# Two layer-norm tiles at a time instead of one on VectorE: subtract, subtract, multiply, multiply

## The chip, the cores and the metric

The kernel runs on all 8 cores of one Trainium2 chip. Each core computes 2048 of the 16384 tokens and talks to no other core; the cores share only the memory behind them. The metric is the device time of the slowest core in microseconds (us).

## The reference

The input is x, 16384 tokens of 4096 features (float32). Two sub-layers follow each other, each wrapped in two layer norms (sandwich form):

```
x = x + layernorm( layernorm(x) @ weight.T + bias )
x = x + layernorm( ffn(layernorm(x)) )
ffn(y) = y @ W_base.T + b_base + 2 * sum over experts of w[t,e] * (y @ lora_A[e].T) @ lora_B[e].T
```

The expert weights w are a softmax over 8 router logits of which the two largest are kept and made to sum to one. The two products with 4096x4096 matrices are nearly all of the arithmetic.

## The kernel before

Features lie on the 128 partitions, tokens along the free dimension. A core works through its 2048 tokens in four chunks of 512 (`ch`), and a chunk is 32 tiles of 128 features by 512 tokens (`k`). `xt` holds x in float32, `u` the normalized input of a product in bf16, `zb` the product in bf16. Each chunk goes through these stages, one after the other:

1. **A, first statistics.** ACT issues four loads of `xt`, 8 tiles each (line 227), copies and squares each tile (lines 233, 234), and PE sums over partitions with a column of ones. The load of the group g of the next chunk waits until POOL has made the output tile 8g+7 of this chunk, since that add reads `xt` (lines 220, 221).
2. **A, apply (lines 266 to 273).** The mean and the inverse deviation are spread over the partitions as `mbc_bf` and `ibc_bf`. VectorE (DVE) subtracts and multiplies tile by tile through two small buffers `ybf0`, `ybf1` and writes `u`. The first product's matmuls of its first output tile wait for `u` tile by tile (line 339).
3. **B, product.** 32 output tiles of 32 matmuls each (line 340), weights through two buffers `wb`. In chunk 0 the float32 weights are cast on the way in and written back to memory as bf16; later chunks read the bf16 copy. ACT copies and squares each result (lines 324, 325).
4. **C, apply and first residual (lines 364 to 374).** For each tile DVE subtracts (`zb` minus mean into `ybf`, line 367) and multiplies in place (line 370), and POOL (GpSimd) adds the result to `xt` (line 373). ACT squares the new `xt` (line 382) for the next statistics.
5. **D, apply (lines 416 to 423).** As in A, into `u`, for the router (line 432) and the second product. Stages A and D are called the u stages below.
6. **E, product.** As in B (line 527), with the low-rank part.
7. **F, apply, second residual and store (lines 549 to 567).** Subtract (line 553), multiply (line 556), add on POOL into one of two float32 buffers `ost` (line 559), and a store of 256 KB by the queue of SP (line 563). With it run the loads and statistics of the next chunk's stage A.

All order between and within engines is by semaphores written by hand. On DVE, a multiply waits for the subtract whose result it reads. In stage C the subtract of tile k waits for the add of tile k-2, in stage F for the add and for the store of tile k-2. POOL's own queue also issues the weight loads, in program order with its adds; the first two of a product stand behind the 32 adds of the stage before it.

Of the kernel before, what the change touches and what calls it, by code (L numbers as in the profile page):

```python
# [14 lines left out]
C = 512  # L15
NCH = TOK // C
KT = D // 128
# [6 lines left out]
def build_nc():  # L24
# [10 lines left out]
    outd = nc.dram_tensor("out", [D, TOK], F32, kind="ExternalOutput").ap()  # L35
# [3 lines left out]
    cnt = {"t": 0, "v": 0, "s": 0, "g": 0, "gc": 0,  # L39
           "x": [0, 0, 0, 0], "w": [0, 0], "o": [0, 0], "wsc": [0, 0]}  # L40

    def emit(e, fn):
        ops[e].append(fn)

    def wait(e, sem, val):
        if val > 0:
            emit(e, lambda eng, sem=sem, val=val: eng.wait_ge(sem, val))

    with ExitStack() as _es:
        xt = _es.enter_context(nc.sbuf_tensor("xt", [128, KT * C], F32))  # L50
        u = _es.enter_context(nc.sbuf_tensor("u", [128, KT * C], BF16))
        zb = _es.enter_context(nc.sbuf_tensor("zb", [128, OC * C], BF16))
# [14 lines left out]
        ybf0 = _es.enter_context(nc.sbuf_tensor("ybf0", [128, C], BF16))  # L67
        ybf1 = _es.enter_context(nc.sbuf_tensor("ybf1", [128, C], BF16))
        mbc_bf = _es.enter_context(nc.sbuf_tensor("mbc_bf", [128, C], BF16))
        ibc_bf = _es.enter_context(nc.sbuf_tensor("ibc_bf", [128, C], BF16))  # L70
# [36 lines left out]
        s_v = _es.enter_context(nc.semaphore("s_v"))  # L107
# [12 lines left out]
        s_gc = _es.enter_context(nc.semaphore("s_gc"))  # L120
# [4 lines left out]
        ost = [ost0, ost1]  # L125
# [3 lines left out]
        s_o = [s_o0, s_o1]  # L129
# [10 lines left out]
        def v_inc(fn):  # L140
            cnt["v"] += 1
            emit("V", lambda v, fn=fn: fn(v).then_inc(s_v, 1))
            return cnt["v"]

        def s_inc(fn):
            cnt["s"] += 1
            emit("S", lambda s, fn=fn: fn(s).then_inc(s_s, 1))
            return cnt["s"]

        def g_inc(fn):  # L150
            cnt["gc"] += 1
            emit("G", lambda g, fn=fn: fn(g).then_inc(s_gc, 1))
            return cnt["gc"]
# [25 lines left out]
        nout = 0  # L179
# [33 lines left out]
        f6k = {}  # L213
        for ch in range(NCH):
            t_pair = {}
            s_pair = {}
            for k in range(KT):
                if k % 8 == 0:
                    g = k // 8
# [43 lines left out]
                wait("V", s_gc, f6k[KT - 1])  # L263
            uk = {}
            yb = [ybf0, ybf1]
            for k in range(KT):
                if k >= 2:
                    wait("V", s_v, uk[k - 2])
                r = v_inc(lambda v, k=k: v.tensor_sub(yb[k % 2][:],  # L269
                                                      xt[:, k * C:(k + 1) * C], mbc_bf[:]))  # L270
                wait("V", s_v, r)
                uk[k] = v_inc(lambda v, k=k: v.tensor_mul(u[:, k * C:(k + 1) * C],  # L272
                                                          yb[k % 2][:], ibc_bf[:]))
            vv_u_done = cnt["v"]
            vv_apply_bank_free = cnt["v"]

# [83 lines left out]
            wait("V", s_o[0], cnt["o"][0])  # L360
            wait("V", s_o[1], cnt["o"][1])
            c3k = {}
            yb = [ybf0, ybf1]
            for k in range(KT):
                if k >= 2:
                    wait("V", s_gc, c3k[k - 2])
                r = v_inc(lambda v, k=k: v.tensor_sub(yb[k % 2][:],  # L367
                                                      zb[:, k * C:(k + 1) * C], mbc_bf[:]))
                wait("V", s_v, r)
                vc = v_inc(lambda v, k=k: v.tensor_mul(yb[k % 2][:], yb[k % 2][:],  # L370
                                                       ibc_bf[:]))
                wait("G", s_v, vc)
                c3k[k] = g_inc(lambda g, k=k: g.tensor_add(  # L373
                    xt[:, k * C:(k + 1) * C], xt[:, k * C:(k + 1) * C], yb[k % 2][:]))
            vv_c_done = cnt["v"]
            vv_apply_bank_free = cnt["v"]

# [22 lines left out]
            r = v_inc(lambda v: v.tensor_scalar_mul(row_a[:], ps_sqq[0:1, :], 1.0 / D))  # L400
            wait("V", s_v, r)
            r = v_inc(lambda v: v.tensor_mul(row_b[:], row_m[:], row_m[:]))
            wait("V", s_v, r)
            r = v_inc(lambda v: v.tensor_sub(row_a[:], row_a[:], row_b[:]))
# [4 lines left out]
            r = s_inc(lambda s: s.activation(row_b[:], row_a[:], AF.Ln))  # L409
# [3 lines left out]

            wait("V", s_s, bc_d)
            wait("V", s_gc, c3k[KT - 1])
            for k in range(KT):
                if k >= 2:
                    wait("V", s_v, uk[k - 2])
                r = v_inc(lambda v, k=k: v.tensor_sub(yb[k % 2][:],  # L419
                                                      xt[:, k * C:(k + 1) * C], mbc_bf[:]))  # L420
                wait("V", s_v, r)
                uk[k] = v_inc(lambda v, k=k: v.tensor_mul(u[:, k * C:(k + 1) * C],  # L422
                                                          yb[k % 2][:], ibc_bf[:]))
            vv_u_done = cnt["v"]
            vv_apply_bank_free = cnt["v"]

# [21 lines left out]
            for tt in range(4):  # L448
# [17 lines left out]
                r2 = v_inc(lambda v, tt=tt: v.reduce_max(m2s[:, tt:tt + 1], l2t[:],  # L466
                                                         axis=AX.X))
# [78 lines left out]
            vv_stats_read = va  # L546
            bc_f = bc_pair(row_zm, va, sa, vv_apply_bank_free, s_free_need=vv_u_done)
            wait("V", s_s, bc_f)
            for k in range(KT):
                if k >= 2:  # L550
                    wait("V", s_o[k % 2], cnt["o"][k % 2])
                    wait("V", s_gc, f6k[k - 2])
                r = v_inc(lambda v, k=k: v.tensor_sub(yb[k % 2][:],  # L553
                                                      zb[:, k * C:(k + 1) * C], mbc_bf[:]))
                wait("V", s_v, r)
                vc = v_inc(lambda v, k=k: v.tensor_mul(yb[k % 2][:], yb[k % 2][:],  # L556
                                                       ibc_bf[:]))
                wait("G", s_v, vc)
                f6k[k] = g_inc(lambda g, k=k: g.tensor_add(  # L559
                    ost[k % 2][:], yb[k % 2][:], xt[:, k * C:(k + 1) * C]))  # L560
                wait("Y", s_gc, f6k[k])
                def ostore(y, ch=ch, k=k):
                    return y.dma_start(outd[k * 128:(k + 1) * 128, ch * C:(ch + 1) * C],
                                       ost[k % 2][:]).then_inc(s_o[k % 2], 16)
                emit("Y", ostore)
                nout += 1
                cnt["o"][k % 2] += 16
            vv_f6_done = cnt["v"]
            sv_zb_free = cnt["v"]
            vv_apply_bank_free = cnt["v"]  # L570
# [84 lines left out]
```

## Time and profile before

| | before |
|---|---|
| median of 3 runs | 3453.99 us (3449.34 to 3455.17) |
| the profiled execution's own time | 3449.01 us |
| its span, first to last instruction (slowest core) | 3447.2 us |
| spans of the 8 cores | 3421.6 to 3447.2 us |
| PE busy | 2386.2 us (69%) |
| DVE busy | 658.0 us (19%) |
| ACT busy | 544.5 us (16%) |
| POOL busy | 441.2 us (13%) |

Busy shares are averages over stages that are limited by different things, so they don't say what a change in one stage is worth. For that one reads the chain of work that ended last, and the timeline of the stage.

### The profile page before, as it was taken

What the parts mean: (1) busy time and instruction counts of PE and PEld (TensorE: products, weight loads), DVE (VectorE), ACT (ScalarE), POOL (GpSimd) and SP (SyncE); (2) the same over time, 40 slices, a digit from 0 to 9 for tenths busy, and PEclk for the clock granted to TensorE, in tenths of its full rate; (3) what the DMA queues carried; (4) which work ended last, traced back from release to release, by engine and by line L of the source; (5) the groups of instructions that cost most, each with busy time, mean ns of one, the idle gap of its engine ahead of it and who ended that gap; (6) DMA issues with size and microseconds to landing.
All of it is one profiled execution on the core that took longest, in us unless ns stands there. A gap on an engine that the chain in (4) does not pass through costs nothing.

```text
span 3447.2 us, 27405 instructions; the slowest of 8 cores (3421.6 to 3447.2 us)
## 1 busy us (share of the span) xinstructions
PE 2386.2 (69%) x10016; PEld 971.7 (28%) x10204; DVE 658.0 (19%) x1243; ACT 544.5 (16%) x1001; POOL 441.2 (13%) x521
## 2 busy tenths in 40 slices
PE   2577853788713998279943899459962599639990
PEld 0133311333300443034410344124420144214440
DVE  0400037000034000820022300640012400370003
ACT  3110121011122111211113011301112111211110
POOL 0000022000030000400022000400013000220004
PEclk7698975899955999589975799669985699759995
DMA  7298932799742333024334234013425144103332
GB/s 173 60 201 200 204 91 51 165 201 209 179 136 84 126 140 112 26 71 144 136 105 143 89 139 145 32 38 137 141 86 171 64 139 141 61 26 126 139 114 98
DMA packets 81891, 417.12 MB, mean 121 GB/s; under 512 B 7648, under 2 KB 7776, under 8 KB 40544
## 3 DMA queue, kind: packets, MB, share of 16 engines
q0 software_dynamic: 37472, 279.04, 30.6%
q1 hardware_dynamic: 27648, 102.77, 7.6%
q10 hardware_dynamic: 16640, 33.56, 3.0%
q8 instruction: 83, 1.36, 0.2%
q14 instruction: 48, 0.39, 0.0%
HBM read 383.98 MB, written 102.76 MB: 141 GB/s over the span
## 4 chain that ended last, share of the span: by engine, by line
PE 48%; DMA 24%; DVE 15%; issue 6%; ACT 3%; POOL 2%; another core or an unknown queue 1%; DVEq 0%; ACTq 0%; POOLq 0%; SPq 0%
PE P L340 21%; PE P L527 21%; DMA wsc<-wb 6%; DMA out<-ost 5%; DMA wb<-wF 5%; DMA wb<-wA 5%; DVE ybf L370 4%; DMA xt<-xT 3%; DVE ybf L419 3%; DVE ybf L269 3%; POOL ost L559 2%; DVE ybf L367 2%; PE ps_sq L306 1%; DVE ybf L556 1%; DVE ybf L553 1%
## 5 line engine op out<-in xcount | busy, mean ns | idle before, releaser
L340 PE MATMUL P<-u,wb 128*128 128x512 bf16 x4004 | 972.1, 394 | 156.6 <-DVE u L272 82.5
L527 PE MATMUL P<-u,wb 128*128 128x512 bf16 x4012 | 930.9, 389 | 74.6 <-DMA wb<-wF 62.5
L340 PEld LDWEIGHTS P<-u,wb 128*128 128x128 bf16 x4096 | 404.4, 100 | 718.5 <-issue 282.8
L527 PEld LDWEIGHTS P<-u,wb 128*128 128x128 bf16 x4096 | 404.5, 100 | 588.1 <-issue 137.9
L324 ACT CAST zb<-P 128x512 bf16<-128x512 f32 x256 | 149.8, 585 | 2019.3 <-PE P L345 790.1
L184 DVE TENSOR_SCALAR row_zm<-ps_sq 1x512 f32<-1x512 f32 x8 | 5.4, 679 | 2163.7 <-PE ps_sqq L312 2163.7
L297 POOL DMA_DIRECT2D wb<-wsc x192 | 101.5, 529 | 1699.4 <-PE P L345 840.8
L242 PE MATMUL ps_sq<-xbf,ones 128*1 128x512 bf16 x128 | 60.1, 569 | 354.2 <-ACT sq L234 354.2
L559 POOL TENSOR_TENSOR ost<-ybf,xt 128x512 f32<-128x512 bf16 x128 | 150.0, 1172 | 328.5 <-DVE ybf L556 328.5
L373 POOL TENSOR_TENSOR xt<-xt,ybf 128x512 f32<-128x512 f32 x128 | 153.3, 1198 | 169.4 <-DVE ybf L370 165.6
L325 ACT ACTIVATE sq<-P 128x512 bf16<-128x512 f32 x256 | 154.4, 603 | 0.0
L370 DVE TENSOR_TENSOR ybf<-ybf,ibc_bf 128x512 bf16<-128x512 bf16 x128 | 148.3, 1158 | 14.8 <-DVE ybf L367 1.8
L389 PE MATMUL ps_sqq<-sq,ones 128*1 128x512 bf16 x64 | 37.4, 585 | 160.2 <-ACT sq L382 160.2
L233 ACT CAST xbf<-xt 128x512 bf16<-128x512 f32 x128 | 77.5, 605 | 290.4 <-DMA xt<-xT 290.0
L432 PE MATMUL ps_mix<-rTs,u 128*128 128x8 bf16 x512 | 31.5, 167 | 132.3 <-DVE u L422 132.3
L242 PEld LDWEIGHTS ps_sq<-xbf,ones 128*1 128x1 bf16 x128 | 7.3, 80 | 408.6 <-issue 408.6
L553 DVE TENSOR_TENSOR ybf<-zb,mbc_bf 128x512 bf16<-128x512 bf16 x128 | 64.3, 503 | 242.5 <-DMA out<-ost 199.9
L382 ACT ACTIVATE sq<-xt 128x512 bf16<-128x512 f32 x128 | 80.7, 630 | 134.8 <-POOL xt L373 125.9
L269 DVE TENSOR_TENSOR ybf<-xt,mbc_bf 128x512 bf16<-128x512 f32 x128 | 87.8, 686 | 28.0 <-ACT ibc_bf L210 27.9
L419 DVE TENSOR_TENSOR ybf<-xt,mbc_bf 128x512 bf16<-128x512 f32 x128 | 87.9, 687 | 26.9 <-ACT ibc_bf L210 26.9
L234 ACT ACTIVATE sq<-xt 128x512 bf16<-128x512 f32 x128 | 79.9, 624 | 0.0
L306 PE MATMUL ps_sq<-zb,ones 128*1 128x512 bf16 x256 | 65.5, 378 | 11.0 <-ACT sq L325 11.0
(87 smaller groups left out, 989.0 us busy)
## 6 DMA issues: line engine op xcount, KB each, us to landing
wb<-wsc POOLq DMA_DIRECT2D x192, 1056.0 KB, 5.3
wsc<-wb SPq DMA_DIRECT2D x64, 1056.0 KB, 7.7
wb<-wA POOLq DMA_DIRECT2D x32, 1056.0 KB, 11.2
wb<-wF POOLq DMA_DIRECT2D x32, 1056.0 KB, 11.3
xt<-xT ACTq DMA_DIRECT2D x16, 2048.0 KB, 10.3
out<-ost SPq DMA_DIRECT2D x128, 256.0 KB, 2.4
aTs<-aT POOLq DMA_DIRECT2D x1, 1024.0 KB, 15.6
bTs<-bT POOLq DMA_DIRECT2D x1, 1024.0 KB, 22.1
```

The lines of the kernel that those rows point to most:

```text
L269: r = v_inc(lambda v, k=k: v.tensor_sub(yb[k % 2][:], xt[:, k * C:(k + 1) * C], mbc_bf[:]))
L297: emit("G", lambda g, mat=mat, oc=oc, par=par: g.dma_start(wb[par][:], wsc[mat, oc]).then_inc(s_w[par], 16))
L306: t_run(lambda t, j=j: t.matmul(ps_sq[0:1, :], ones128[:, 0:1], zb[:, j * C:(j + 1) * C], start=(j == 0), stop=(j == OC - 1)))
L324: s_inc(lambda s, po=po: s.copy(zb[:, po * C:(po + 1) * C], P[po % 2][:]))
L325: ev[po] = s_inc(lambda s, po=po: s.activation(sq[po % 4][:], P[po % 2][:], AF.Square))
L340: t_run(lambda t, oc=oc, k=k: t.matmul(P[oc % 2][:], wb[oc % 2][:, k * 128:(k + 1) * 128], u[:, k * C:(k + 1) * C], start=(k == 0), stop=F ...
L370: vc = v_inc(lambda v, k=k: v.tensor_mul(yb[k % 2][:], yb[k % 2][:], ibc_bf[:]))
L373: c3k[k] = g_inc(lambda g, k=k: g.tensor_add(xt[:, k * C:(k + 1) * C], xt[:, k * C:(k + 1) * C], yb[k % 2][:]))
L419: r = v_inc(lambda v, k=k: v.tensor_sub(yb[k % 2][:], xt[:, k * C:(k + 1) * C], mbc_bf[:]))
L527: t_run(lambda t, oc=oc, k=k: t.matmul(P[oc % 2][:], wb[oc % 2][:, k * 128:(k + 1) * 128], u[:, k * C:(k + 1) * C], start=(k == 0), stop=F ...
L553: r = v_inc(lambda v, k=k: v.tensor_sub(yb[k % 2][:], zb[:, k * C:(k + 1) * C], mbc_bf[:]))
L559: f6k[k] = g_inc(lambda g, k=k: g.tensor_add(ost[k % 2][:], yb[k % 2][:], xt[:, k * C:(k + 1) * C]))
```

## The change

In the four apply loops the 32 tiles are taken in 16 pairs (`kp`). DVE subtracts both tiles of a pair (into `ybf0` and `ybf1`), waits for the second subtract, and multiplies both. Before the next pair it waits for what used the two buffers last: in the u stages for the pair's second multiply; in stage C for POOL's add of the pair's second tile; in stage F for that add and for the stores of both tiles. The instructions, their shapes and their buffers are the same; their order on DVE and the waits differ. The order on POOL and SP is the same.

```diff
 # stages A and D (two loops of this form)
-            for k in range(KT):
-                if k >= 2:
-                    wait("V", s_v, uk[k - 2])
-                r = v_inc(lambda v, k=k: v.tensor_sub(yb[k % 2][:],
-                                                      xt[:, k * C:(k + 1) * C], mbc_bf[:]))
-                wait("V", s_v, r)
-                uk[k] = v_inc(lambda v, k=k: v.tensor_mul(u[:, k * C:(k + 1) * C],
-                                                          yb[k % 2][:], ibc_bf[:]))
+            for kp in range(0, KT, 2):
+                if kp >= 2:
+                    wait("V", s_v, uk[kp - 1])
+                v_inc(lambda v, kp=kp: v.tensor_sub(yb[0][:],
+                                                    xt[:, kp * C:(kp + 1) * C], mbc_bf[:]))
+                r2 = v_inc(lambda v, kp=kp: v.tensor_sub(
+                    yb[1][:], xt[:, (kp + 1) * C:(kp + 2) * C], mbc_bf[:]))
+                wait("V", s_v, r2)
+                uk[kp] = v_inc(lambda v, kp=kp: v.tensor_mul(
+                    u[:, kp * C:(kp + 1) * C], yb[0][:], ibc_bf[:]))
+                uk[kp + 1] = v_inc(lambda v, kp=kp: v.tensor_mul(
+                    u[:, (kp + 1) * C:(kp + 2) * C], yb[1][:], ibc_bf[:]))
 # stage F (stage C has the same form, without the stores and their waits)
-            for k in range(KT):
-                if k >= 2:
-                    wait("V", s_o[k % 2], cnt["o"][k % 2])
-                    wait("V", s_gc, f6k[k - 2])
-                r = v_inc(lambda v, k=k: v.tensor_sub(yb[k % 2][:],
-                                                      zb[:, k * C:(k + 1) * C], mbc_bf[:]))
-                wait("V", s_v, r)
-                vc = v_inc(lambda v, k=k: v.tensor_mul(yb[k % 2][:], yb[k % 2][:],
-                                                       ibc_bf[:]))
-                wait("G", s_v, vc)
-                f6k[k] = g_inc(lambda g, k=k: g.tensor_add(
-                    ost[k % 2][:], yb[k % 2][:], xt[:, k * C:(k + 1) * C]))
...
+            for kp in range(0, KT, 2):
+                if kp >= 2:
+                    wait("V", s_o[0], cnt["o"][0])
+                    wait("V", s_o[1], cnt["o"][1])
+                    wait("V", s_gc, f6k[kp - 1])
+                v_inc(lambda v, kp=kp: v.tensor_sub(yb[0][:],
+                                                    zb[:, kp * C:(kp + 1) * C], mbc_bf[:]))
+                r2 = v_inc(lambda v, kp=kp: v.tensor_sub(
+                    yb[1][:], zb[:, (kp + 1) * C:(kp + 2) * C], mbc_bf[:]))
+                wait("V", s_v, r2)
+                vc0 = v_inc(lambda v: v.tensor_mul(yb[0][:], yb[0][:], ibc_bf[:]))
+                vc1 = v_inc(lambda v: v.tensor_mul(yb[1][:], yb[1][:], ibc_bf[:]))
+                for k, vc in ((kp, vc0), (kp + 1, vc1)):
+                    wait("G", s_v, vc)
+                    f6k[k] = g_inc(lambda g, k=k: g.tensor_add(
+                        ost[k % 2][:], yb[k % 2][:], xt[:, k * C:(k + 1) * C]))
...
```

## Rows read from the trace of the kernel before

**Rows 1.** Spans and mean granted TensorE clock, the slowest core:
```profile
core 6: 3447.2 us, clock 0.814
```
**Rows 2.** Page: the chain that ended last, by engine; then waits (total, times, longest):
```profile
PE 48%; DMA 24%; DVE 15%; issue 6%; ACT 3%; POOL 2%; another core or an unknown queue 1%; DVEq 0%; ACTq 0%; POOLq 0%; SPq 0%
...
DVE ybf L553 <- DMA out<-ost: 199.9, 98, 6.5
...
POOL xt L373 <- DVE ybf L370: 165.6, 121, 31.7
...
PE ps_mix L432 <- DVE u L422: 132.3, 128, 2.8
```
**Rows 3.** Engines in stage C of chunk 1 (busy PE, PEld, DVE, ACT, POOL; PEclk; DMA):
```profile
1378.00:1431.00 53.00, 15.17 (x30) 1.70 (x30) 47.95 (x64) 19.69 (x32) 37.99 (x32) 0.50 0.00 1
```
**Rows 4.** Timeline, stage A apply of chunk 1 (start us, us, engine line):
```profile
1108.23 0.68 DVE L269 TENSOR_TENSOR ybf<-xt,mbc_bf 128x512 bf16<-128x512 f32 x1
...
1108.46 0.59 PE L340 MATMUL P<-u,wb 128*128 128x512 bf16 x1 [0.55 <-DVE u L272]
1109.02 0.42 DVE L272 TENSOR_TENSOR u<-ybf,ibc_bf 128x512 bf16<-128x512 bf16 x1
1109.36 0.69 DVE L269 TENSOR_TENSOR ybf<-xt,mbc_bf 128x512 bf16<-128x512 f32 x1
```
**Rows 5.** Timeline, stage C of chunk 1, its start and its end:
```profile
1378.39 0.43 DVE L367 TENSOR_TENSOR ybf<-zb,mbc_bf 128x512 bf16<-128x512 bf16 x1 [6.76 <-ACT ibc_bf L210]
1378.92 0.43 DVE L370 TENSOR_TENSOR ybf<-ybf,ibc_bf 128x512 bf16<-128x512 bf16 x1
1379.27 0.42 DVE L367 TENSOR_TENSOR ybf<-zb,mbc_bf 128x512 bf16<-128x512 bf16 x1
1379.50 1.19 POOL L373 TENSOR_TENSOR xt<-xt,ybf 128x512 f32<-128x512 f32 x1 [27.97 <-DVE ybf L370]
1379.79 1.19 DVE L370 TENSOR_TENSOR ybf<-ybf,ibc_bf 128x512 bf16<-128x512 bf16 x1
1380.79 0.63 ACT L382 ACTIVATE sq<-xt 128x512 bf16<-128x512 f32 x1 [2.63 <-POOL xt L373]
1380.90 0.41 DVE L367 TENSOR_TENSOR ybf<-zb,mbc_bf 128x512 bf16<-128x512 bf16 x1
1381.12 1.20 POOL L373 TENSOR_TENSOR xt<-xt,ybf 128x512 f32<-128x512 f32 x1 [0.42 <-DVE ybf L370]
...
1430.17 1.15 POOL L373 TENSOR_TENSOR xt<-xt,ybf 128x512 f32<-128x512 f32 x1 [0.42 <-PE ps_sqq L392]
1431.27 1.09 POOL L297 DMA_DIRECT2D wb<-wsc  x2
```
**Rows 6.** Stage C's adds in chunk 1 (ns min/median/max, first to last start us):
```profile
L373 POOL TENSOR_TENSOR xt<-xt,ybf x32: 1150/1201/1203, 1379.5 to 1430.2; 128x512 f32<-128x512 f32 x32
```
**Rows 7.** Timeline, stage F of chunk 1: an add and the subtract after its store:
```profile
1768.66 1.16 POOL L559 TENSOR_TENSOR ost<-ybf,xt 128x512 f32<-128x512 bf16 x1 [1.91 <-DVE ybf L556]
...
1772.68 0.43 DVE L553 TENSOR_TENSOR ybf<-zb,mbc_bf 128x512 bf16<-128x512 bf16 x1 [2.06 <-DMA out<-ost]
```
**Rows 8.** Stage F's adds in the four chunks (as in group 6):
```profile
L559 POOL TENSOR_TENSOR ost<-ybf,xt x32: 1154/1157/1428, 959.7 to 1050.4; 128x512 f32<-128x512 bf16 x32
...
L559 POOL TENSOR_TENSOR ost<-ybf,xt x32: 1154/1158/1420, 1764.0 to 1854.1; 128x512 f32<-128x512 bf16 x32
...
L559 POOL TENSOR_TENSOR ost<-ybf,xt x32: 1154/1158/1396, 2562.9 to 2662.8; 128x512 f32<-128x512 bf16 x32
...
L559 POOL TENSOR_TENSOR ost<-ybf,xt x32: 1154/1157/1202, 3368.8 to 3443.1; 128x512 f32<-128x512 bf16 x32
```
**Rows 9.** The stores of stage F of chunk 3, issue to landing:
```profile
DMA to landing us min/median/max: 2.1/2.2/2.7
```
**Rows 10.** A load of `xt` (timeline), and a piece of the chain in chunk 1:
```profile
1782.70 0.43 ACTq L227 DMA_DIRECT2D xt<-xT  x1
...
1785.22 6.76 DMA out<-ost
```

More of the change, by code:

```diff
@@ L362, in build_nc @@
             c3k = {}
-            yb = [ybf0, ybf1]
-            for k in range(KT):
-                if k >= 2:
-                    wait("V", s_gc, c3k[k - 2])
-                r = v_inc(lambda v, k=k: v.tensor_sub(yb[k % 2][:],
-                                                      zb[:, k * C:(k + 1) * C], mbc_bf[:]))
-                wait("V", s_v, r)
-                vc = v_inc(lambda v, k=k: v.tensor_mul(yb[k % 2][:], yb[k % 2][:],
-                                                       ibc_bf[:]))
-                wait("G", s_v, vc)
-                c3k[k] = g_inc(lambda g, k=k: g.tensor_add(
-                    xt[:, k * C:(k + 1) * C], xt[:, k * C:(k + 1) * C], yb[k % 2][:]))
+            for kp in range(0, KT, 2):
+                if kp >= 2:
+                    wait("V", s_gc, c3k[kp - 1])
+                v_inc(lambda v, kp=kp: v.tensor_sub(yb[0][:],
[7 more added lines that the diff above has]
+                    wait("G", s_v, vc)
+                    c3k[k] = g_inc(lambda g, k=k: g.tensor_add(
+                        xt[:, k * C:(k + 1) * C], xt[:, k * C:(k + 1) * C],
+                        yb[k % 2][:]))
             vv_c_done = cnt["v"]
@@ L415, in build_nc @@
             wait("V", s_gc, c3k[KT - 1])
[L416 to L423, printed above, removed]
+            for kp in range(0, KT, 2):
+                if kp >= 2:
+                    wait("V", s_v, uk[kp - 1])
+                v_inc(lambda v, kp=kp: v.tensor_sub(yb[0][:],
+                                                    xt[:, kp * C:(kp + 1) * C], mbc_bf[:]))
+                r2 = v_inc(lambda v, kp=kp: v.tensor_sub(
+                    yb[1][:], xt[:, (kp + 1) * C:(kp + 2) * C], mbc_bf[:]))
+                wait("V", s_v, r2)
+                uk[kp] = v_inc(lambda v, kp=kp: v.tensor_mul(
+                    u[:, kp * C:(kp + 1) * C], yb[0][:], ibc_bf[:]))
+                uk[kp + 1] = v_inc(lambda v, kp=kp: v.tensor_mul(
+                    u[:, (kp + 1) * C:(kp + 2) * C], yb[1][:], ibc_bf[:]))
             vv_u_done = cnt["v"]
@@ L548, in build_nc, with ostore @@
             wait("V", s_s, bc_f)
-            for k in range(KT):
-                if k >= 2:
-                    wait("V", s_o[k % 2], cnt["o"][k % 2])
-                    wait("V", s_gc, f6k[k - 2])
[L553 to L558, printed above, removed]
-                f6k[k] = g_inc(lambda g, k=k: g.tensor_add(
-                    ost[k % 2][:], yb[k % 2][:], xt[:, k * C:(k + 1) * C]))
[L561 to L567, printed above, removed]
+            for kp in range(0, KT, 2):
+                if kp >= 2:
+                    wait("V", s_o[0], cnt["o"][0])
+                    wait("V", s_o[1], cnt["o"][1])
+                    wait("V", s_gc, f6k[kp - 1])
+                v_inc(lambda v, kp=kp: v.tensor_sub(yb[0][:],
+                                                    zb[:, kp * C:(kp + 1) * C], mbc_bf[:]))
+                r2 = v_inc(lambda v, kp=kp: v.tensor_sub(
+                    yb[1][:], zb[:, (kp + 1) * C:(kp + 2) * C], mbc_bf[:]))
+                wait("V", s_v, r2)
+                vc0 = v_inc(lambda v: v.tensor_mul(yb[0][:], yb[0][:], ibc_bf[:]))
+                vc1 = v_inc(lambda v: v.tensor_mul(yb[1][:], yb[1][:], ibc_bf[:]))
+                for k, vc in ((kp, vc0), (kp + 1, vc1)):
+                    wait("G", s_v, vc)
+                    f6k[k] = g_inc(lambda g, k=k: g.tensor_add(
+                        ost[k % 2][:], yb[k % 2][:], xt[:, k * C:(k + 1) * C]))
+                    wait("Y", s_gc, f6k[k])
+                    def ostore(y, ch=ch, k=k):
+                        return y.dma_start(
+                            outd[k * 128:(k + 1) * 128, ch * C:(ch + 1) * C],
+                            ost[k % 2][:]).then_inc(s_o[k % 2], 16)
+                    emit("Y", ostore)
+                    nout += 1
+                    cnt["o"][k % 2] += 16
```

## The prediction

> **What bounds the kernel now.** I first read the spans of the cores: the slowest is core 6, and all rows are its own [rows 1]. Then the chain that ended last: PE has only half of it, DMA and DVE most of the rest [rows 2]. So the kernel runs in phases: in the products PE is the bound, and between them PE waits for the layer norms. The waits name the phases that the change touches. POOL waits 165.6 us for DVE's multiply in stage C, DVE waits 199.9 us for stores in stage F, and PE waits 132.3 us for `u` at the router [rows 2]. In stage C's window nothing covers this: PE is at clock 0.50, its lower level (1.2 GHz), with 15 of 53 us busy on small sums, DMA moves nothing, and DVE and POOL alternate [rows 3]. All four apply loops lie on the path, so what a loop loses, the kernel loses. The rest of the reading is the timeline of each loop, from which I build the loop anew in the new order.
>
> **Three prices of DVE.** A DVE instruction that needs nothing from the one before it starts 0.08 us before that one's end: the multiply at 1378.92 is followed by the subtract at 1379.27, 0.35 us from start to start. One that needs its result starts 0.10 us after the end: 1378.39 to 1378.92, 0.53 us [rows 5]. So a true wait on the previous instruction costs 0.18 us. The same in the u stages: 0.79 us from a float32 subtract to its multiply, 0.34 us from there to the next subtract [rows 4].
>
> **The u stages (A and D, 8 loops).** Before, a pair of tiles takes 2 x (0.79 + 0.34) = 2.26 us. After, second subtract: the trace has no two float32 subtracts in a row; by the overlap of 0.08 it starts 0.60 us after the first. Then 0.79 to the first multiply, 0.34 to the second, and now the next pair waits for that multiply: 0.53. Sum 2.26 us. The pairing removes one true wait per pair (between a subtract and its multiply) and adds one (between the second multiply and the next subtract), since only two buffers exist. Gain: zero; only the last pair has no next one, 0.19 us per loop. PE's matmul on a new tile runs at the low clock (0.59 us for one [rows 4]; its 512 columns alone are 0.43 at 1.2 GHz), longer than the 0.34 between the two multiplies, which takes back about 0.09 at the end. Together -0.1 x 8, about -1 us. Bounds: if two subtracts don't overlap, +0.19 x 16 pairs x 8 loops = +24 us; nothing can gain more than the -1.5 of the last pairs unless a wait is free.
>
> The Trainium skill (VectorE: DVE Perf Modes, "The DRAIN you can't avoid") says that leaving semaphores out between DVE instructions saves nothing, because each drains the pipeline anyway. By it the second subtract would start 0.53 and not 0.35 us after the first, and the change would cost some 23 us more in stages C and F together. The trace disagrees: 0.35 against 0.53 in two neighbouring steps [rows 5].
>
> **Stage C (4 loops).** Before, DVE and POOL run in a chain: multiply ends, add starts 0.14 us later, meanwhile the next subtract runs; the next multiply is recorded from 1379.79 for 1.19 us, of which only the last 0.29 lie behind the add; then the next add [rows 5]. Per tile 1.20 + 0.43; the 31 steps take 50.7 us [rows 6], 3.27 us per pair. The subtract is hidden under this; the multiply nearly so. After, DVE may not start a pair before POOL has made both adds, so nothing hides any longer. One pair:
> - from the add's end to the subtract: 0.10, as ACT needs it (add ends 1380.69, ACT starts 1380.79) [rows 5];
> - subtract to subtract 0.35, subtract to multiply 0.53, multiply to first add 0.58 (1378.92 to 1379.50) = 1.46; the second multiply starts 0.35 after the first, as the subtract does now, and ends before the first add does;
> - first add 1.20, of which 0.05 is waiting for the DVE instruction begun before it (an undisturbed one takes 1.15), second add right behind: POOL's next instruction starts 1.10 after an add of 1.15 began [rows 5], so 1.15 to the second's start and 1.15 to its end = 2.30.
>
> Together 3.86 us against 3.27. From first to last add 15 x 3.86 + 1.15 = 59.0 us against 50.7: +8.4 per loop, +33.5 in all (chunk 0's loop is 0.3 shorter before). Behind the adds in POOL's queue stand the first two weight loads of stage E; they move with the stage and still have the whole of stage D before the first matmul needs them. ACT's squares take 0.63 and keep up. Bounds: if the first add must wait for the whole second multiply, 0.15 more per pair; if the second add starts later by a handshake of 0.14, as much again; below, 0.10 less if DVE starts with no delay. That is 27 to 50 us.
>
> **Stage F (4 loops).** Chunk 3's loop has no loads beside it: 74.3 us for 31 steps [rows 8], 4.79 us per pair. A buffer's loop is subtract to multiply 0.53, multiply to add 0.58, add 1.16, and then the store; what is left for the store with its issue and both handshakes is 4.79 - 2.27 = 2.52 us. It fits the landing of 2.2 us [rows 9], and the single case beside other stores from 1769.82 to 1772.68, 2.86 us [rows 7]. Before, two such loops run interleaved. After, both wait for the later store, and the two adds stand one behind the other: 1.46 + 2.30 + 2.52 = 6.28 us per pair. Loop: 15 x 6.28 + 1.15 = 95.4 us against 74.3: +21.0 for chunk 3. With 2.86 for the store it would be +26, with 2.35 it would be +18.5.
>
> Chunks 0 to 2 have three loads of `xt` inside the loop; their loops take 90.7, 90.1 and 99.9 us [rows 8], so a load costs (90.4 - 74.3) / 3 = 5.4 us before in the first two. The mechanism is in one row: a store issued 2.5 us behind a load takes 6.76 us and lands 9.3 after the load's issue [rows 10]. After, the pair behind the load makes its adds later: 2.5 + 1.46 + 2.30 = 6.3 us after the load's issue, and its last store would land at 8.8 anyway. So it loses 0.5 us at least, and 4.3 if it also takes 6.76. I take 2 per load, since only the tail of the load is met: 95.4 + 6 = 101.4, and 7 more in chunk 2, where some other contention adds about 10 now. Against 90.7, 90.1 and 99.9: +10.7, +11.3, +8.5 = +30.3 (the third with 108.4). With no loss and nothing in chunk 2 it would be +5; with the old price 5.4 and chunk 2's whole excess +63.
>
> The loads of the next chunk move with the adds; the last one is issued after the last add in either kernel, and the statistics after it are as before. Chunk 0's weight casts and write-backs, and all products, are shifted and not changed.
>
> **Sum.** -1 + 33.5 + 21.0 + 30.3 = +83.8 us. On the profiled execution, 3449.0 us (span 3447.2), that gives 3532.8; the median of the runs lies 5.0 above it, so 3454.0 + 83.8 = 3537.8, rounded to 3538: slower by 2.4%.
>
> **Rivals.**
> 1. *The port between DVE and POOL is freed, and the kernel gets faster.* Now nearly every multiply of stage C stretches beside an add, 1.19 for 0.43 us (POOL waits for one 121 times) [rows 2, 5]; with DVE silent during the adds that stretching goes, about 0.75 x 121 = 90 us of DVE's busy time. For it to bring time, the add itself must get faster, because the stretched part lies beside an add. Place: the adds of stages C and F. The pairing costs 84 us over 256 adds, so it decides at 0.33 us per add, 1.15 down to 0.82; at 0.80 the kernel would take 3538 - 0.35 x 256 = 3448. Against it: the shortest of all adds, some of them with DVE idle, takes 1.15 [rows 6, 8]. The Trainium skill (SBUF — State Buffer, "Who interferes with whom") has the port as an exclusive lock whose loser is blocked; the row of the multiply that ends 0.29 behind the add agrees. By that rule the first add of a pair would wait out the second multiply, which makes the change dearer by 19 us.
> 2. *Stage F hides it.* If stores bunched in pairs meet the loads less and a load costs nothing, and the wait for the store shrinks to the shortest, 2.35, each loop takes 15 x 6.11 + 1.15 = 92.8 us; chunks 0 to 2 then lose 2.1 and 2.7 and gain 7.1, chunk 3 loses 18.5, about +16 together, and with stage C's 33.5 the time is 3503. For it: the third loop's 99.9 us shows how much is contention. Against: the stores' wait is now serial for both buffers.
> 3. *Everything at its dear end.* No overlap of float32 subtracts (+24), old price of loads (+33): 3454 + 84 + 57 = 3595. Against it: the overlap shows in every bf16 step.
> 4. *No change that can be measured*: it would need DVE's waits in C and F to be met already. They can't be: the add waited for is the last that POOL made.
>
> **How the numbers follow.** Forecast as summed with its bounds, 3510 to 3585: 0.80. Rival 2 (3485 to 3510): 0.10. Rival 3 (over 3585): 0.07. Rival 1: 0.02 faster. Rival 4: 0.01. The range that leaves out no more than two in ten is that of the forecast, 3510 to 3585. 0.2% is about what a measurement of this kernel can tell from no change. Faster 0.02, same 0.01, slower 0.97.
>
> **What would show it.** In the timeline of stage C, pairs of adds back to back with a gap of about 1.55 us between pairs, a pair every 3.9 us, and multiplies of 0.43. In stage F, a pair every 6.3 us and over 2.4 us from the second add's end to the subtract. In the u stages the same 36 us. All three products unchanged. Wrong if adds of a pair are apart, if the first-to-last add of a stage C loop is below 55 us, if a float32 subtract starts 0.79 and not 0.60 after the one before, or if a load in stage F costs its old 5.4 us.

## The result, and the profile after

| | before | after |
|---|---|---|
| median | 3454.58 us (10 runs) | 3551.16 us (10 runs) |
| ratio after to before, 95% interval | | 1.027 (1.0242 to 1.0299) |
| the profiled execution's own time | 3449.01 us | 3553.48 us |
| its span, slowest core | 3447.2 us, core 6 | 3551.9 us, core 1 |

The medians differ by 96.6 us, and the ratio gives 93; 83.8 were forecast. Some executions of any of these kernels run some per cent longer, with the cores of one die at a lower granted clock, and the medians take them in while the ratios and their intervals leave them out. The top of the page after, with the busy times and the chain that ended last:

```profile
span 3551.9 us, 27097 instructions; the slowest of 8 cores (3518.9 to 3551.9 us)
## 1 busy us (share of the span) xinstructions
PE 2385.1 (67%) x10204; PEld 971.6 (27%) x10204; DVE 531.1 (15%) x1243; ACT 544.5 (15%) x1001; POOL 434.1 (12%) x521
...
PE 48%; DMA 22%; DVE 14%; issue 7%; POOL 5%; ACT 3%; DVEq 0%; POOLq 0%; ACTq 0%; SPq 0%
```

DVE has the same 1243 instructions and is busy for 531.1 us instead of 658.0, while the kernel takes longer. Most of the 127 us were instructions that stretched beside an add and were hidden there, the multiplies of stage C above all. This row of the page before has them at 1158 ns each; after, none takes over 0.43 us, which alone is 94 us less:

```profile
L370 DVE TENSOR_TENSOR ybf<-ybf,ibc_bf 128x512 bf16<-128x512 bf16 x128 | 148.3, 1158 | 14.8 <-DVE ybf L367 1.8
```

POOL's share of the chain rose from 2% [rows 2] to 5%: its adds no longer run beside the work of DVE for the next tile.

The waits after (total, times, longest), to be read against [rows 2]:

```profile
DVE ybf L565 <- DMA out<-ost: 318.8, 60, 8.0
...
POOL xt L379 <- DVE ybf L375: 205.2, 61, 32.2
...
DVE ybf L370 <- POOL xt L379: 134.4, 60, 2.6
...
PE ps_mix L443 <- DVE u L431: 119.5, 64, 3.4
```

DVE's wait for stores grew from 199.9 to 318.8 us, and there is a wait that the kernel before did not have: DVE for POOL's second add in stage C, 60 times 2.2 us. The timeline of stage C of chunk 1 after, one pair and the start of the next:

```profile
1424.99 0.43 DVE L370 TENSOR_TENSOR ybf<-zb,mbc_bf 128x512 bf16<-128x512 bf16 x1 [2.22 <-POOL xt L379]
1425.34 0.42 DVE L372 TENSOR_TENSOR ybf<-zb,mbc_bf 128x512 bf16<-128x512 bf16 x1
...
1425.86 0.42 DVE L375 TENSOR_TENSOR ybf<-ybf,ibc_bf 128x512 bf16<-128x512 bf16 x1
...
1426.20 0.42 DVE L376 TENSOR_TENSOR ybf<-ybf,ibc_bf 128x512 bf16<-128x512 bf16 x1
1426.43 2.31 POOL L379 TENSOR_TENSOR xt<-xt,ybf 128x512 f32<-128x512 f32 x2 [1.54 <-DVE ybf L375]
...
1428.84 0.42 DVE L370 TENSOR_TENSOR ybf<-zb,mbc_bf 128x512 bf16<-128x512 bf16 x1 [2.22 <-POOL xt L379]
```

Four DVE instructions of 0.42 us run while POOL stands idle for 1.54 us; then two adds back to back, 2.31 us, while DVE stands idle for 2.22. A pair every 3.85 us. In [rows 5] POOL's gap is 0.42 us per tile. The u stages, of which this is the start of stage D in chunk 1, and one step of stage F in chunk 3:

```profile
1494.72 0.69 DVE L426 TENSOR_TENSOR ybf<-xt,mbc_bf 128x512 bf16<-128x512 f32 x1 [6.72 <-ACT ibc_bf L210]
1495.33 0.69 DVE L428 TENSOR_TENSOR ybf<-xt,mbc_bf 128x512 bf16<-128x512 f32 x1
1496.12 0.43 DVE L431 TENSOR_TENSOR u<-ybf,ibc_bf 128x512 bf16<-128x512 bf16 x1
1496.46 0.42 DVE L433 TENSOR_TENSOR u<-ybf,ibc_bf 128x512 bf16<-128x512 bf16 x1
1496.98 0.69 DVE L426 TENSOR_TENSOR ybf<-xt,mbc_bf 128x512 bf16<-128x512 f32 x1
```

```profile
3455.43 2.32 POOL L574 TENSOR_TENSOR ost<-ybf,xt 128x512 f32<-128x512 bf16 x2 [28.63 <-DVE ybf L570]
...
3460.12 0.42 DVE L565 TENSOR_TENSOR ybf<-zb,mbc_bf 128x512 bf16<-128x512 bf16 x1 [4.50 <-DMA out<-ost]
...
3461.55 2.32 POOL L574 TENSOR_TENSOR ost<-ybf,xt 128x512 f32<-128x512 bf16 x2 [3.81 <-DVE ybf L570]
```

In the u stages two float32 subtracts start 0.61 us apart, and the next pair starts 0.52 after the second multiply: 2.26 us per pair, as before. In stage F 2.37 us pass between the end of the adds and the next subtract, and a pair comes every 6.12 us. Last, the adds of one stage C and of the four stages F (ns min/median/max, first to last start in us), against [rows 6, 8]:

```profile
L379 POOL TENSOR_TENSOR xt<-xt,ybf x32: 1144/1152/1201, 1422.6 to 1482.0; 128x512 f32<-128x512 f32 x32
```

```profile
L574 POOL TENSOR_TENSOR ost<-ybf,xt x32: 1147/1179/1212, 974.5 to 1095.3; 128x512 f32<-128x512 bf16 x32
...
L574 POOL TENSOR_TENSOR ost<-ybf,xt x32: 1147/1158/1213, 1814.8 to 1916.4; 128x512 f32<-128x512 bf16 x32
...
L574 POOL TENSOR_TENSOR ost<-ybf,xt x32: 1147/1160/1215, 2632.6 to 2738.9; 128x512 f32<-128x512 bf16 x32
...
L574 POOL TENSOR_TENSOR ost<-ybf,xt x32: 1147/1157/1208, 3455.4 to 3547.9; 128x512 f32<-128x512 bf16 x32
```

From first to last add, stage C takes 59.4 us against 50.7. Stage F on core 1: 120.8, 101.6, 106.3 and 92.5 us. Core 1 is the slowest core after, core 6 was the slowest before, so the loops of stage F are better compared over all cores. Each number here is the last add's start minus the first's, as in the rows, taken for each of the 8 cores and averaged (us):

| stage F | chunk 0 | 1 | 2 | 3 | sum |
|---|---|---|---|---|---|
| before | 89.2 | 89.8 | 93.1 | 75.8 | 347.9 |
| after | 109.7 | 104.1 | 103.2 | 94.0 | 410.9 |

Stage F costs 63.0 us more on an average core. The four loops of stage C, taken in the same way, sum to 236.7 us against 202.5, 34.2 more (58.9 to 59.5 each, against 50.4 to 50.7). Together that is 97.2 us. The products are unchanged: a matmul takes 395 and 388 ns on average in the two of them, against 394 and 389.

### The profile page after: what moved, and what is told of

Same layout as the page of the kernel before. It is cut to its first block, busy times and chain, and to the rows that moved or that the text cites. A ratio compares the mean times of both kernels' runs of the same rounds, so it can differ in the third digit from the quotient of the medians.

```text
span 3551.9 us, 27097 instructions; the slowest of 8 cores (3518.9 to 3551.9 us)
## 1 busy us (share of the span) xinstructions
PE 2385.1 (67%) x10204; PEld 971.6 (27%) x10204; DVE 531.1 (15%) x1243; ACT 544.5 (15%) x1001; POOL 434.1 (12%) x521
## 4 chain that ended last, share of the span: by engine, by line
PE 48%; DMA 22%; DVE 14%; issue 7%; POOL 5%; ACT 3%; DVEq 0%; POOLq 0%; ACTq 0%; SPq 0%
PE P L538 21%; PE P L344 20%; DMA wsc<-wb 5%; DMA out<-ost 5%; DMA wb<-wF 5%; DMA wb<-wA 4%; DMA xt<-xT 3%; POOL xt L379 3%; POOL ost L574 3%; PE ps_sq L310 1%; DVE ybf L426 1%; DVE ybf L269 1%; DVE ybf L271 1%; DVE ybf L428 1%; PE ps_sqq L314 1%
## 5 line engine op out<-in xcount | busy, mean ns | idle before, releaser
L565 DVE TENSOR_TENSOR ybf<-zb,mbc_bf 128x512 bf16<-128x512 bf16 x64 | 27.2, 425 | 345.4 <-DMA out<-ost 318.8
L290 POOL DMA_DIRECT2D wb<-wA x32 | 16.9, 531 | 436.3 <-PE P L349 324.4
L443 PEld LDWEIGHTS ps_mix<-rTs,u 128*128 128x128 bf16 x512 | 23.6, 104 | 144.2 <-issue 144.2
## 6 DMA issues: line engine op xcount, KB each, us to landing
wb<-wF POOLq DMA_DIRECT2D x32, 1056.0 KB, 11.3
```

## The experiments

Nine of the eleven kernels were also timed beside the kernel before on the same chip; ratios are to that. Of the two of experiment 6 there is one execution each. Every kernel keeps the whole computation. The code cuts leave out lines that did not change or that repeat the same edit.

**1. Each part alone.** Three kernels take the changed loops in the u stages only (A and D), in stage C only, and in stage F only; the other loops are those before.

> Only the u stages (A and D) are paired; C and F are as before. Theory (one true wait removed per pair, one added): a pair of tiles takes 2.26 us as before, each loop about 0.2 us shorter, the kernel within 2 us of before (3453). Rival A (float32 subtracts don't overlap): +0.19 x 16 x 8 = +24 us, 3479. Rival B (fewer handshakes are a gain in themselves: a wait on DVE's own last multiply costs nothing): -0.19 x 16 x 8 = -24 us, 3431.

> Only stage C is paired. Theory (nothing of DVE lies under POOL's adds any longer): a pair every 3.86 us, first to last add 59 us against 50.7, kernel +33.5 us (3488). Rival (freed port makes the adds faster): adds below 1.10 us each and a kernel of 3454 or less.

> Only stage F is paired. As predicted: chunk 3's loop 95 us against 74, the others 101 to 108, +51 us (3506). By the traces since seen (loops summed over the 8 cores: +63 us a core, with loops of 100 to 120 us in chunk 0): +60 to +70, 3515 to 3524. Rival (stage F hides it in the landing times): below +20.

| kernel | median | ratio (95% interval) | in us by the ratio |
|---|---|---|---|
| u stages only | 3451.89 | 0.999 (0.9958 to 1.0021) | -3 |
| stage C only | 3485.57 | 1.0094 (1.0073 to 1.0115) | +32.5 |
| stage F only | 3516.28 | 1.0182 (1.0156 to 1.0208) | +63 |

The parts add up to +92, and the whole change measured +93 by its ratio. The u stages are worth nothing. That is what the theory said, and it speaks against both rivals (+24 and -24 us): the interval reaches from -14 to +7 us, and the 2.26 us per pair in the trace is sharper. With stage C alone the adds of chunk 1 read

```profile
L376 POOL TENSOR_TENSOR xt<-xt,ybf x32: 1140/1152/1252, 1386.8 to 1446.0; 128x512 f32<-128x512 f32 x32
```

The loop takes 59.2 us. The shortest add takes 1.14 us where it took 1.15 before, and the middle one 1.15 where it took 1.20 [rows 6]: with DVE silent an add gains about 0.05 us, where the rival needed 0.33.

**2. The changed order, but each buffer waited for on its own.**

```diff
 # on the changed kernel; stage F in the same way with its stores
             for kp in range(0, KT, 2):
                 if kp >= 2:
-                    wait("V", s_gc, c3k[kp - 1])
+                    wait("V", s_gc, c3k[kp - 2])
                 v_inc(lambda v, kp=kp: v.tensor_sub(yb[0][:], ...
+                if kp >= 2:
+                    wait("V", s_gc, c3k[kp - 1])
                 r2 = v_inc(lambda v, kp=kp: v.tensor_sub(
```

> The changed kernel, but in C and F each subtract of a pair waits only for what used its own buffer last (the first no longer waits for the second tile's add and store). Theory: the first subtract leaves the path but stays blocked under the second add, so stage C gains about 0.24 us per pair (first to last add 55.5 us) and stage F 0.35 per pair: -35 us against the changed kernel, 3516, still 60 us slower than before. Rival (the doubled wait alone is the loss, and the order of the instructions is not): back to the time before, 3454.

Measured 3517.06 us, ratio 1.0182 (1.0154 to 1.021). That is 34 us less than the changed kernel by the medians and 30 by the ratios, where 35 were expected. From its timeline:

```profile
1423.80 2.31 POOL L382 TENSOR_TENSOR xt<-xt,ybf 128x512 f32<-128x512 f32 x2 [1.29 <-DVE ybf L378]
1425.11 1.29 DVE L371 TENSOR_TENSOR ybf<-zb,mbc_bf 128x512 bf16<-128x512 bf16 x1 [1.11 <-POOL xt L382]
...
1426.32 0.41 DVE L375 TENSOR_TENSOR ybf<-zb,mbc_bf 128x512 bf16<-128x512 bf16 x1
...
1427.40 2.31 POOL L382 TENSOR_TENSOR xt<-xt,ybf 128x512 f32<-128x512 f32 x2 [1.29 <-DVE ybf L378]
```

The first subtract may now start when the first add is done, but it stretches to 1.29 us and ends 0.29 after the second add. So a pair takes 3.60 us, 0.25 less, and stage F sums to 385.4 us over the four loops on an average core, 25 less. Two thirds of the loss stay (63 of 93 us by the ratios), so the doubled wait is the smaller part of it. In the rows above POOL still waits 1.29 us between two pairs of adds: for the last 0.29 of the blocked subtract, for the second subtract and for the first multiply. With two buffers none of that can be done earlier.

**3. The changed order over four buffers.** All four loops take pairs; `ybf` and `ost` get four buffers each, and the waits go back two pairs.

```diff
 # against the changed kernel, stage C; in stage F the stores' waits go back in the same way
+                b0, b1 = yb4[kp % 4], yb4[kp % 4 + 1]
-                if kp >= 2:
-                    wait("V", s_gc, c3k[kp - 1])
+                if kp >= 4:
+                    wait("V", s_gc, c3k[kp - 3])
```

> The changed order (subtract, subtract, multiply, multiply) in all four loops, but with four ybf and four ost buffers, so that a pair waits for what the pair before the last one did. Theory (the loss is the reuse of two buffers within one step, not the order): u stages 2.07 us per pair instead of 2.26, -24 us against before; stage C back to about 3.3 us per pair (51 us per loop), bound by POOL and DVE taking turns; stage F no longer waits for landings, about 3.3 to 3.6 us per pair, 25 us or more shorter per loop than before. Kernel 3320 to 3360. Rival (the order itself is the loss: a pair's adds come in a bunch behind four DVE instructions): stage C stays at 58 to 60 us per loop and the kernel above 3440.

Ratio 0.9703 (0.9595 to 0.9811); the two executions that it stands on took 3347 and 3379 us, and the second is the one in the trace. Its stage C in the slowest core, core 4 (DVE, then POOL, then the 32 adds of chunk 2):

```profile
1362.26 1.38 DVE L382 TENSOR_TENSOR ybf<-zb,mbc_bf 128x512 bf16<-128x512 bf16 x1
1363.56 1.37 DVE L384 TENSOR_TENSOR ybf<-zb,mbc_bf 128x512 bf16<-128x512 bf16 x1
1365.04 0.42 DVE L387 TENSOR_TENSOR ybf<-ybf,ibc_bf 128x512 bf16<-128x512 bf16 x1
1365.38 0.42 DVE L388 TENSOR_TENSOR ybf<-ybf,ibc_bf 128x512 bf16<-128x512 bf16 x1
```

```profile
1362.15 2.50 POOL L391 TENSOR_TENSOR xt<-xt,ybf 128x512 f32<-128x512 f32 x2 [0.96 <-DVE ybf L387]
1365.60 2.50 POOL L391 TENSOR_TENSOR xt<-xt,ybf 128x512 f32<-128x512 f32 x2 [0.95 <-DVE ybf L387]
```

```profile
L391 POOL TENSOR_TENSOR xt<-xt,ybf x32: 1147/1226/1332, 2123.6 to 2176.4; 128x512 f32<-128x512 f32 x32
```

Both subtracts of the next pair lie under the adds again, all but the last 0.28 us. The pair takes 3.45 us and the loop 52.8 (52.7 to 53.0 on every core and in every chunk), against 50.7 before and 59.4 after. So in stage C the order alone costs about 2 us per loop; the other 6.4 come from two buffers for a pair, which leave nothing to prepare. The u stages take 2.07 us per pair, as expected. The stage F loops take 69.1, 68.8, 68.8 and 55.1 us on an average core. Here the order is not tested by itself, since the four `ost` buffers alone change much: with them and the old order experiment 5 has 60.1, 58.4, 58.6 and 51.4 us. Whether the 4 to 10 us between the two come from the order or from the store's wait, which stays on DVE here, no run separates.

**4. Where the waits are, seen from the other side.** If a true wait on DVE's previous instruction costs 0.18 us, staggering must gain what pairing over two buffers can't: the subtract of the next tile is put between a subtract and its multiply. The kernel before, u stages only (instructions shortened to words):

```diff
-            for k in range(KT):
-                if k >= 2:
-                    wait("V", s_v, uk[k - 2])
-                r = v_inc(subtract tile k into yb[k % 2])
-                wait("V", s_v, r)
-                uk[k] = v_inc(multiply yb[k % 2] into u, tile k)
+            for k in range(KT + 1):
+                if k < KT:
+                    if k >= 4:
+                        wait("V", s_v, uk[k - 4])
+                    rk[k] = v_inc(subtract tile k into yb4[k % 4])
+                if k >= 1:
+                    wait("V", s_v, rk[k - 1])
+                    uk[k - 1] = v_inc(multiply yb4[(k - 1) % 4] into u, tile k - 1)
```

> The kernel before, but in the u stages the subtract of tile k+1 is issued ahead of the multiply of tile k, over four buffers; C and F as before. Theory (each true wait on DVE's previous instruction costs 0.18 us, and pairing over two buffers only moved it): no wait is true any longer, 0.60 + 0.34 = 0.94 us per tile instead of 1.13, -6 us per loop, -48 us: 3406. Rival (waits cost nothing, DVE is bound by its instructions): 3454.

```profile
1104.75 0.70 DVE L274 TENSOR_TENSOR ybf<-xt,mbc_bf 128x512 bf16<-128x512 f32 x1
1105.35 0.43 DVE L279 TENSOR_TENSOR u<-ybf,ibc_bf 128x512 bf16<-128x512 bf16 x1
1105.69 0.70 DVE L274 TENSOR_TENSOR ybf<-xt,mbc_bf 128x512 bf16<-128x512 f32 x1
1106.29 0.43 DVE L279 TENSOR_TENSOR u<-ybf,ibc_bf 128x512 bf16<-128x512 bf16 x1
```

0.60 + 0.34 = 0.94 us per tile, as expected. From first subtract to last multiply a loop takes 29.7 us against 35.9, which is 50 us in the eight loops. The two executions that the ratio stands on took 3397 and 3399 us, and the trace's own is 52 us below the kernel before; the ratio is 0.9804 (0.9708 to 0.9899), that is -68 us, with an interval from -101 to -35 that holds the 48 expected. Shown: with the same instructions, a wait for the instruction just before costs 0.18 us, and a wait for one further back, which is over by then, costs nothing that these rows can tell.

**5. Stage F's store.** The kernel before, with the store's wait moved from DVE's subtract to POOL's add, and the same with four `ost` buffers.

```diff
                 if k >= 2:
-                    wait("V", s_o[k % 2], cnt["o"][k % 2])
                     wait("V", s_gc, f6k[k - 2])
...
                 wait("G", s_v, vc)
+                wait("G", s_o[k % 2], cnt["o"][k % 2])
```

> The kernel before, but in stage F POOL's add waits for the store of two tiles ago, and not DVE's subtract. Theory (the loop of a buffer, subtract 0.53 + multiply 0.58 + add 1.16 + store 2.52, sets stage F): subtract and multiply leave it, 3.7 us per pair instead of 4.79, chunk 3's loop 57 us against 74, the kernel -50 to -70 us: 3384 to 3404. Rival (the stores' transfer itself is the bound): 3454.

> As f_poolwait, with four ost buffers. Theory: the landing leaves the path altogether, stage F runs at stage C's pace of 3.27 us per pair, 51 us per loop in chunk 3 and somewhat more beside the loads: 3340 to 3370. If the landings still bound it beside the loads of xt: 3370 to 3395.

Measured 3399.74 us, ratio 0.9793 (0.9697 to 0.9888), and 3344.27 us, ratio 0.9648 (0.9587 to 0.9709). The four loops sum to 290.5 and 228.6 us on an average core, against 347.9. Stage F of chunk 3 with four buffers:

```profile
L565 POOL TENSOR_TENSOR ost<-ybf,xt x32: 1152/1157/1387, 3284.8 to 3336.2; 128x512 f32<-128x512 bf16 x32
```

The loop takes 51.4 us, near stage C's pace of 50.7. So before the change the landing of a store was on the path of nearly every tile, and the stage had 23 us per loop to give back even without loads.

**6. Stage F without the loads.** In the kernel before and in the changed one, all loads of `xt` are issued after the last add (`f6k[8 * g + 7]` becomes `f6k[KT - 1]` at line 221). Only the loops are read.

> The kernel before, with all four loads of xt of the next chunk issued after the last add of stage F instead of three of them inside it. Only stage F's loops are read (the kernel as a whole gets slower, the loads no longer lie beside the stage). Theory: the loads are what makes the loops of chunks 0 to 2 longer than chunk 3's: all four loops take 73 to 76 us from first to last add, against 87 to 100 now. Rival (other cores' traffic): chunks 0 to 2 stay 5 us or more longer than chunk 3.

> The changed kernel, with the loads of xt issued after stage F in the same way. Theory: all four loops 92 to 94 us, so that without loads the pairing costs 18 to 19 us per loop in every chunk, and the difference to 100 to 105 now is the price of three loads, about 3 us each against 5 before. If the loops of 115 to 120 us that some cores show in chunk 0 come from the loads, they go too; if they come from two cores that store at the same time, they stay.

| stage F, mean over cores | chunk 0 | 1 | 2 | 3 |
|---|---|---|---|---|
| before, late loads | 72.8 | 74.5 | 73.2 | 73.6 |
| after, late loads | 96.7 | 96.2 | 94.0 | 93.4 |

Before, the difference between the chunks goes with the loads: (90.7 - 73.5) / 3 = 5.7 us per load, where 90.7 is the mean of chunks 0 to 2 before and 73.5 that of the late loops. After, 28 of the 32 loops take 92 to 95.5 us, 93.8 on average. So the pairing costs 20 us per loop without loads, where 18 to 19 were expected, and a load costs (103.6 - 93.8) / 3 = 3.3 us, with 103.6 the mean of chunks 1 and 2 after. But four loops of 100 to 105 us stay, on cores 4 and 5 in chunk 0 and on cores 0 and 1 in chunk 1. The stores of core 4 in its slow chunk 0 and in chunk 1:

```profile
DMA to landing us min/median/max: 2.7/3.1/5.4
...
DMA to landing us min/median/max: 2.1/2.2/3.0
```

In the slow loop the quickest store lands 0.6 us later and the middle one 0.9. No load runs in either, so long loops of this kind come about without loads. They are 11 us longer than the others here and 14 to 19 in chunk 0 of the changed kernel; one execution can't tell whether the loads have a part in that difference.

**7. The two gains together.** Experiment 4's u stages and experiment 5's stage F with four `ost` buffers, stage C as before.

> The kernel before, with the staggered subtracts and multiplies over four ybf buffers in the u stages, and in stage F the store's wait on POOL with four ost buffers; stage C as before. The two gains lie in different stages and should add: -110 and -50 to -57 us: 3290 to 3300. If either only opened a wait that the other one closes: above 3310.

Measured 3295.09 us, ratio 0.9532 (0.951 to 0.9555): 4.7% faster than the kernel before and 7% faster than the changed one. The time is the forecast one, so within the noise the gains added: the ratios of the two parts multiply to 0.946, and the intervals of those two are wide enough for the difference.

## Why the prediction was right

**The three prices of DVE held.** In the timelines after, a subtract follows a subtract by 0.35 us (float32 0.61, forecast 0.60), and a multiply follows the subtract it waits for by 0.52 (float32 0.79). Experiment 4 has 0.60 + 0.34.

**U stages, forecast -1 us.** 2.26 us per pair, as summed; alone they measured -3 within its interval. The bound of +24 (subtracts that don't overlap) is excluded by the row of 0.61.

**Stage C, forecast 3.86 us per pair and +33.5.** 3.85 us, 59.4 us per loop against the 59.0 forecast, +34.2 in the four loops and +32.5 alone. The gap of POOL was to be 1.55 and is 1.54.

**Stage F, forecast +51.3, measured +63.0 on an average core; the mechanism was right, the size in part by luck.** As forecast, both tiles wait for the later store and the adds stand behind each other. (The three differences +10.7, +11.3 and +8.5 add up to 30.5, not 30.3, which changes nothing.) For core 6, on which it was worked out, the sum fits: 102.3, 106.7, 106.2 and 94.1 us after, against the forecast of 101.4, 101.4, 108.4 and 95.4, in sum +54. But core 6 was not an average core before. Its four loops sum to 355.0 us against 347.9, most of it the 99.9 us of chunk 2. That is 7 of the 12 us by which the forecast was too small. The other 4 to 5 are what is left of four errors that went both ways, 406.6 us forecast for the four loops after and 410.9 measured:
- A load costs 3.3 us in the new order and not 2, about 4 us a chunk in three chunks: +11.
- In chunk 0 four cores have loops of 116 to 121 us beside four with 100 to 103. The forecast had no such loss: +6 on average.
- The loop without loads takes 93.8 us and not 95.4, mainly since a pair takes 6.12 us and not 6.28 (the wait for the store is 2.37 and not 2.52): -6 in four loops.
- The 7 us that the forecast added in chunk 2 for "some other contention" did not come: chunk 2 takes 103.2 us and chunk 1 104.1. That excess stood in the one execution on cores 0, 1, 6 and 7 (95 to 100 us beside 87 to 91) and does not belong to the chunk: -7.

**The rivals.** The freed port was the one to fear, since 127 us of DVE's busy time did go. It brought next to nothing: the middle add of stage C fell from 1.20 to 1.15 us, the length that the forecast had already given to an undisturbed one, and no add in these traces is shorter than 1.14. Stage F did not hide the change: alone it costs 63 us. The dear end of everything did not come either: float32 subtracts do overlap, and a load costs less than it did.

**The Trainium skill.** VectorE: DVE Perf Modes, "The DRAIN you can't avoid", says of eight copies in a row that a semaphore after each costs nothing extra. Here a wait that is true costs 0.18 us per instruction, and removing one per tile in the u loops gave experiment 4 its ratio of 0.98; the measurement decides. The same section adds that a next instruction which isn't held (made to wait for all earlier ones) starts earlier, so the forecast read the rule more strictly than it stands there; the steps of 0.35 and 0.53 us put a number to the difference. SBUF — State Buffer, "Who interferes with whom", says that the port pair between DVE and GpSimd is an exclusive lock; the subtracts of 1.29 and 1.38 us in experiments 2 and 3 agree. Read as a lock for the whole instruction, it would have delayed the first add of a pair by the 0.19 us that the second multiply (1426.20, 0.42 long) still runs when the add starts at 1426.43. That did not come: the first add of a pair takes 1.20 us in the middle and the second 1.15, so 0.05 us is lost.

## What to carry to other kernels

Grouping independent instructions removes a wait only if the next group has other buffers; with two buffers for a pair it moves the wait to the pair's end and makes it longer, because two engines that took turns on one tile now take turns on two. Before regrouping a loop between two engines, write down for one period what runs under what, and count the buffers that leave something to prepare. Take the loop's present length from all cores and not from one, since one core can carry an excess that isn't the loop's own. Put a wait on the engine that needs it (the store's on the add), not on one two steps ahead. A fall in an engine's busy time says nothing if the time was stretched under another engine's work.

## What was unexpected

In stage F some loops are longer on both cores of a neighbouring pair (0 and 1, 2 and 3, and so on) than on the rest. After the change these are cores 0, 1, 4 and 5 in chunk 0 (116 to 121 us beside 100 to 103). With stage F alone they are cores 2 and 3 in chunk 0 (122 and 117) and 6 and 7 in chunk 3 (103 and 102 beside 94), and with late loads the four named above. The kernel before has them too: cores 4 and 5 in chunk 3 (81 beside 74), and cores 0, 1, 6 and 7 in chunk 2 (95 to 100 beside 87 to 91), the excess that the prediction took for chunk 2's own. There the middle store lands after 2.7 and 2.8 us where it takes 2.1 to 2.4 on the others, and after 2.8 to 3.1 where it takes 2.3 to 2.6. The price is 5 to 19 us in the paired order and 5 to 11 in the old one. That two cores which store in step hold each other up would explain the pairs. But in experiment 5 with two `ost` buffers core 4 alone has 84 to 85 us in chunks 0 to 2 where core 5 has 75 to 80, the traces of two cores have no common clock, and no run controlled it. So the cause stays open.
